# Attention scores of two units at a time as float32 matmuls in the two row halves of TensorE's array, with the step's order on TensorE rewritten

## The reference

```python
q = layernorm(x); k = v = ctx
scores = einsum('bsgrd,btgd->bgrst', xq, xk) / sqrt(64) + mask      # 224 x 750 for each of 8 x 32 heads
probs = softmax(scores)
x = x + tanh(g_xattn) * einsum('bgrst,btgd->bsgrd', probs, xv)
x = x + tanh(g_ffn) * ffn(layernorm(x))                            # routed values, gate from a small MLP
```

## Time and profile before

| | |
|---|---|
| median of 3 runs | 1175.29 us |
| profiled execution | 1174.98 us |
| its span | 1173.1 us |
| TensorE (matmuls) busy | 1150.5 us, 98% |
| VectorE busy | 947.2 us, 81% |
| ScalarE busy | 912.7 us, 78% |
| GpSimd busy | 889.6 us, 76% |
| granted TensorE clock | 0.999 of full |

### The profile page before, as it was taken

How to read it: one execution, slowest core, us unless ns; L and a number is a source line. 1 busy time by engine, 2 the same in 40 slices (tenths; PEclk the granted TensorE clock), 3 DMA queues, 4 the chain that set the end, 5 groups by cost and what they waited for, 6 DMA issues and landing times.

```text
span 1173.1 us, 35389 instructions
## 1 busy us (share of the span) xinstructions
PE 1150.5 (98%) x14656; PEld 907.2 (77%) x14656; DVE 947.2 (81%) x2269; ACT 912.7 (78%) x1226; POOL 889.6 (76%) x804
## 2 busy tenths in 40 slices
PE   5999999999999999999999999999999999999997
PEld 3888888888888888888888888888887655655553
DVE  5888888888888888888888888888874899676775
ACT  5899898888898888898899988898881444655544
POOL 6899999999999999999999999999992110314222
PEclk9999999999999999999999999999999999999999
DMA  9421231133114212411331131122126500012224
GB/s 337 150 69 48 57 117 42 55 75 106 41 43 107 80 49 53 121 42 55 69 111 42 42 73 52 48 53 57 43 79 187 234 2 1 1 59 87 108 99 153
DMA packets 60735, 95.09 MB, mean 81 GB/s; under 512 B 35233, under 2 KB 44449, under 8 KB 56482
## 3 DMA queue, kind: packets, MB, share of 16 engines
q1 hardware_dynamic: 59858, 91.79, 25.7%
q10 hardware_dynamic: 720, 1.05, 0.3%
HBM read 71.75 MB, written 20.97 MB: 79 GB/s over the span
## 4 chain that ended last, share of the span: by engine, by line
PE 76%; POOL 20%; DMA 1%; DVE 1%; issue 1%; ACT 1%; DVEq 0%; SPq 0%; POOLq 0%
POOL arena L593 14%; PE psum L988 13%; PE psum L912 12%; PE psum L935 12%; PE psum L942 6%; PE psum L923 6%; PE psum L965 5%; PE psum L959 5%; PE psum L960 5%; PE psum L1069 3%; POOL arena L560 2%; PE psum L975 2%; PE psum L890 2%; POOL arena L613 1%; PE psum L1038 1%; POOL arena L601 1%
## 5 line engine op out<-in xcount | busy, mean ns | idle before, releaser
L593 POOL TENSOR_TENSOR arena<-arena 128x768 bf16<-128x768 f32 x448 | 651.6, 1469 | 39.7 <-ACT arena L722 37.1
L1312 DVE CUSTOM_DVE_ANT_0 arena<-psum,arena 128x750 f32<-128x750 f32 x448 | 420.3, 938 | 127.1 <-PE psum L923 121.4
L722 ACT ACTIVATE arena<-psum 128x768 f32<-128x768 f32 x448 | 362.3, 809 | 89.4 <-PE psum L942 89.3
L726 ACT ACTIVATE arena<-arena,neg_max 128x750 f32<-128x750 f32 x448 | 410.9, 917 | 3.8 <-DVE neg_max L1312 3.7
L912 PE MATMUL psum<-arena 128*128 128x512 bf16 x896 | 272.1, 384 | 0.8 <-DVE arena L1209 0.8
L935 PE MATMUL psum<-ident,arena 128*128 128x128 f32 x1792 | 268.4, 272 | 0.0
L959 PEld LDWEIGHTS psum<-arena 128*128 128x128 bf16 (+1 forms) x2688 | 194.7, 98 | 57.5
L960 PE MATMUL psum<-arena 128*128 128x64 bf16 (+1 forms) x2688 | 222.0, 193 | 0.0
L959 PE MATMUL psum<-arena 128*128 128x65 bf16 (+1 forms) x2688 | 221.7, 194 | 0.0
L960 PEld LDWEIGHTS psum<-arena 128*128 128x128 bf16 (+1 forms) x2688 | 178.5, 98 | 53.2
L935 PEld LDWEIGHTS psum<-ident,arena 128*128 128x128 f32 x1792 | 206.3, 140 | 4.3
(11 more groups left out here) (166 smaller groups left out, 1301.3 us busy)
## 6 DMA issues: line engine op xcount, KB each, us to landing
arena<-in_k_t SPq DMA_DIRECT2D x128, 187.5 KB, 3.2
arena<-in_v_rows SPq DMA_DIRECT2D x64, 192.0 KB, 2.5
out<-arena SPq DMA_DIRECT2D x12, 1024.0 KB, 3.9
arena<-in_x_top SPq DMA_DIRECT2D x8, 1024.0 KB, 5.4
arena<-in_x_rest SPq DMA_DIRECT2D x8, 768.0 KB, 4.6
spill<-arena SPq DMA_DIRECT2D x96, 64.0 KB, 2.2
arena<-spill SPq DMA_DIRECT2D x6, 1024.0 KB, 10.6
arena<-in_w_t SPq DMA_DIRECT2D x4, 1024.0 KB, 20.4
```

The lines of the kernel that those rows point to most:

```text
L593: pool.tensor_tensor(p_lo[:, n % RING, :], p_sb[:, n % RING, :], high(p_sb[:, n % RING, :]), ALU.subtract).then_inc(p_split, 1)
L722: act.activation(p_sb[:, n % RING, :], flat_ps[:, turned_at(n):turned_at(n) + CW], ACT.Copy).then_inc(evac_a, 1)
L726: act.activation(s_sb[:, n % RING, 0:CTX], s_sb[:, n % RING, 0:CTX], ACT.Exp, bias=neg_max[:, n % 4, :], scale=-1.0).then_inc(exped, 1)
L1312: dve.tensor_tensor_reduce(s_sb[:, n % RING, 0:CTX], flat_ps[:, score_at(n):score_at(n) + CTX], mask_sb[:, max(n % UNITS - REP + 1, 0), :] ...
```

## The change

The scores are now done for two units, a and a+1 (a even), at once, as float32 matmuls without any splitting. The query buffer holds float32, head 2i of a pair of units in rows 0 to 63 and head 2i+1 in rows 64 to 127, as the transposition leaves them; each unit uses one half of the rows as its stationary operand (64 rows), and the copy of the keys that lies in the same rows. The 750 columns of each unit are cut in three steps (238, 274, 238), so placed that at no step the two halves write the same bank; the last block of the odd unit, in bank 1, waits for the even unit's first one (`middle_written`). `k_lo` and its buffer use, `split_k`, `split_q`, `round_q` and their semaphores go; VectorE makes one full-height copy of the turned queries in place of two half copies and two subtractions, for the first pair of groups ScalarE does. So that the units of the second group of each pair find their keys and queries in the same half, the units of that group are taken in exchanged order of heads (`m ^ g % 2`), and the second gathered block is written crossed by two instructions (`crossed`).

TensorE's step is: transposition of unit k+2; in even steps, the scores of units k+4 and k+5; the values of unit k. The odd step has no scores. The scores wait for `maxed` of both units of the pair before. VectorE's reduction waits for both units of its pair. Of each 14 evacuations two (n mod 14 in 1 and 7) go from ScalarE to VectorE.

```diff
+DVE_EVACS = (1, 7)
 def evac_on_dve(n):
-    return False
+    return n % (2 * UNITS) in DVE_EVACS
...
-        k_lo = carve("attention", [128, 2, CTX], BF16)
+        carve("attention", [128, CTX])
-        q_t = carve("attention", [128, 2, 2, UNITS, 128], BF16)
+        q_t = carve("attention", [128, 2, UNITS, 128])
...
+        SCORE_STEPS = ((slice(512, 750), slice(238, 476)), (slice(0, 274), slice(476, 750)), (slice(274, 512), slice(0, 238)))
...
-            def split_k(g):
-                pool.wait_ge(k_loaded[g % 2], 32 * (g // 2 + 1))
-                if g >= 2:
-                    pool.wait_ge(scored, UNITS * (g - 1))
-                pool.tensor_tensor(k_lo[:, g % 2, :], k_raw[:, g % 2, :], high(k_raw[:, g % 2, :]),
-                                   ALU.subtract).then_inc(k_split, 1)
...
+            def score_pair(a):
+                pair, at = divmod(a, 2 * UNITS)
+                for n in (a, a + 1):
+                    g = n // UNITS
+                    if n % UNITS == 0:
+                        pe.wait_ge(k_loaded[g % 2], 32 * (g // 2 + 1))
+                if pair == 0 and at in (0, REP, REP + 2):
+                    pe.wait_ge(q_first, {0: 1, REP: 2, REP + 2: 3}[at])
+                if pair >= 1 and at in (0, REP + 2):
+                    pe.wait_ge(q_copied, 2 * pair - 1 if at == 0 else 2 * pair)
+                if a >= 2:
+                    pe.wait_ge(maxed, a)
+                for i, step in enumerate(SCORE_STEPS):
+                    for half in range(2):
+                        n = a + half
+                        rows, cols = slice(D * half, D * half + D), step[half]
+                        if i == 2 and half == 1:
+                            pe.wait_ge(middle_written, a // 2 + 1)
+                        mm = pe.matmul(flat_ps[:, score_at(n) + cols.start:score_at(n) + cols.stop], q_t[rows, pair % 2, turned_slot(n), :],
+                                       k_raw[rows, n // UNITS % 2, cols], start=True, stop=True)
+                        if i == 0 and half == 0:
+                            mm.then_inc(middle_written, 1)
+                        if i == 2:
+                            mm.then_inc(scored, 1)
...
                 if 0 <= k + 2 < NU:
                     turn_main(k + 2)
                     turn_mid(k + 2)
-                if 0 <= k + 5 < NU:
-                    score_main(k + 5)
+                if k % 2 == 0 and 0 <= k + 4 < NU:
+                    score_pair(k + 4)
                 if k >= 0:
                     value(k)
...
-                if 0 <= k + 5 < NU:
-                    score_mid(k + 5)
-                if k + 5 == 0:
+                if k + 4 == 0:
...
-                    dve.wait_ge(scored, n + 1)
+                    dve.wait_ge(scored, n // 2 * 2 + 2)
+                    if n % 2 == 1 and n >= RING:
+                        dve.wait_ge(turned, n - RING + 1)
...
-                    for half in range(2):
-                        dve.tensor_copy(q_t[D * half:D * half + D, pair % 2, half, turns[0]:turns[-1] + 1, :],
-                                        mix_ps[D * half:D * half + D, (window + 1) % 2, 0:128 * len(turns)].rearrange("p (t n) -> p t n", n=128)
-                                        ).then_inc(q_hi_own, 1)
-                if m in (4, 5) and 1 <= pair < PAIRS:
-                    split_q((window + 1) % 2, pair, m - 4, turn_range(window), 2 * (window + 3) + m - 4 + 1)
+                    dve.tensor_copy(q_t[:, pair % 2, turns[0]:turns[-1] + 1, :],
+                                    mix_ps[:, (window + 1) % 2, 0:128 * len(turns)].rearrange("p (t n) -> p t n", n=128)).then_inc(q_copied, 1)
```

More of the change, by code:

```diff
@@ L61, in evac_on_dve @@
 def evac_on_dve(n):
-    return False
+    return n % (2 * UNITS) in DVE_EVACS
 def evacs_before(n, on_dve):
-    whole, part = divmod(n, UNITS)
-    return sum(whole + (1 if m < part else 0) for m in range(UNITS) if evac_on_dve(m) == on_dve)
+    whole, part = divmod(n, 2 * UNITS)
+    return sum(whole + (1 if m < part else 0) for m in range(2 * UNITS) if evac_on_dve(m) == on_dve)
 def flamingo_block(nc, x_top, x_rest, k_t, v_rows, mask, g_x, av_t, wvd_t, w1_t, wq_t, wr, wr_rows_in, keys_t, log_rel, rel, b1, w2, wvu_t,
@@ L256, in flamingo_block @@
         v_loaded = [sem("v_loaded0"), sem("v_loaded1")]
-        k_split = sem("k_split")
         v_hi_done = sem("v_hi_done")
@@ L260, in flamingo_block @@
         q_turned = sem("q_turned")
-        q_hi_done = sem("q_hi_done")
-        q_hi_own = sem("q_hi_own")
-        q_split = sem("q_split")
+        q_first = sem("q_first")
+        q_copied = sem("q_copied")
+        middle_written = sem("middle_written")
         scored = sem("scored")
@@ L354, in turned_slot, with crossed @@
             if m < REP:
-                return m % 2, (0 if u == 0 else 5) + m // 2
-            return u, 2 + (m - REP)
+                return (0 if u == 0 else 5) + m // 2
+            return 2 + (m - REP)
+        def crossed(cols):
+            return cols.rearrange("p (q a d) -> p q a d", a=2, d=D)
         def turn_range(window):
@@ L362, in flamingo_block @@
         FIRST_BANK = (1, 0, 1)
-        def queries_before(pair):
-            return 4 * pair + 2 if pair else 0
         def evac_wait(eng, n):
@@ L579, in _ @@
             factors(0, top_col)
-            split_k(0)
             root(1, rest_cols)
@@ L585, in _ @@
                 for j in range(NB):
-                    pool.tensor_scalar(xn_rest[:, j, cols], xb[:, 0, j, cols], ln_scale[:, 1 + j:2 + j], ln_bias[:, 1 + j:2 + j],
-                                       ALU.mult, ALU.add).then_inc(done, 1)
+                    scale, bias = ln_scale[:, 1 + j:2 + j], ln_bias[:, 1 + j:2 + j]
+                    if j == 1:
+                        dst, src = crossed(xn_rest[:, j, cols]), crossed(xb[:, 0, j, cols])
+                        pool.tensor_scalar(dst[:, :, 1, :], src[:, :, 0, :], scale, bias, ALU.mult, ALU.add)
+                        pool.tensor_scalar(dst[:, :, 0, :], src[:, :, 1, :], scale, bias, ALU.mult, ALU.add).then_inc(done, 1)
+                    else:
+                        pool.tensor_scalar(xn_rest[:, j, cols], xb[:, 0, j, cols], scale, bias, ALU.mult, ALU.add).then_inc(done, 1)
             for k in range(FIRST, NU):
@@ L594, in _ @@
                                        ALU.subtract).then_inc(p_split, 1)
-                g = window + 2
-                if m == 5 and 1 <= g < GROUPS:
-                    split_k(g)
                 g = window + 1
@@ L694, in norm_rest @@
                 act.wait_ge(ln_done, b + 2)
-                act.activation(xn_rest[:, j, :], xb[:, b % 3, j, :], ACT.Identity, bias=ln_bias[:, 1 + j:2 + j],
-                               scale=ln_scale[:, 1 + j:2 + j]).then_inc(rest_normed, 1)
+                scale, bias = ln_scale[:, 1 + j:2 + j], ln_bias[:, 1 + j:2 + j]
+                if j == 1:
+                    dst, src = crossed(xn_rest[:, j, :]), crossed(xb[:, b % 3, j, :])
+                    act.activation(dst[:, :, 1, :], src[:, :, 0, :], ACT.Identity, bias=bias, scale=scale)
+                    act.activation(dst[:, :, 0, :], src[:, :, 1, :], ACT.Identity, bias=bias, scale=scale).then_inc(rest_normed, 1)
+                else:
+                    act.activation(xn_rest[:, j, :], xb[:, b % 3, j, :], ACT.Identity, bias=bias, scale=scale).then_inc(rest_normed, 1)
             def round_h(t, j):
@@ L702, in round_h, with copy_first @@
                 act.activation(h_hi[:, j], psum[:, j % 2, :].rearrange("p (k n) -> p k n", k=4), ACT.Copy).then_inc(h_hi_done, 1)
[L704 to L710, removed]
-                for half in range(2):
-                    round_q(FIRST_BANK[i], 0, half, FIRST_TURNS[i], i + 1)
+            def copy_first(i):
+                turns = FIRST_TURNS[i]
+                act.wait_ge(q_turned, i + 1)
+                act.activation(q_t[:, 0, turns[0]:turns[-1] + 1, :],
+                               mix_ps[:, FIRST_BANK[i], 0:128 * len(turns)].rearrange("p (t n) -> p t n", n=128), ACT.Copy).then_inc(q_first, 1)
             norm_top(0)
-            round_first(0)
+            copy_first(0)
             for k in range(FIRST, NU):
@@ L739, in _ @@
                 if k in (-3, -2):
-                    round_first(k + 4)
+                    copy_first(k + 4)
                 later = (window - 3) // KV + 1
@@ L862, in turn_first @@
                 if i == 2:
-                    pe.wait_ge(q_split, 2)
+                    pe.wait_ge(q_first, 1)
                 turn_rows(0, FIRST_TURNS[i], FIRST_BANK[i])
@@ L875, in turn_q @@
                     pe.wait_ge(rest_widened, NB)
-                    pe.wait_ge(q_split, 6)
+                    pe.wait_ge(q_first, 3)
                 if window >= 1:
@@ L951, in value @@
                         pe.wait_ge(x_added, g - 1)
-                    pe.wait_ge(q_split, min(2 * g + 6, 4 * PAIRS + 2) if g else 4)
+                    if g == 0:
+                        pe.wait_ge(q_first, 2)
```

(16 more changed lines are left out.)

## The result

The changed kernel takes 1389.37 us (median, 1389.03 to 1389.75), the kernel before beside it 1175.08; the ratio is 1.182, 95% interval 1.180 to 1.184. The profiled execution has a span of 1386.0 us and a granted clock of 1.00. The forecast was 1426 us with a range of 1310 to 1680.

A forecast was written before the change was run, and what follows sets the result against it. TensorE's order was taken to bound the kernel before, a loop over three engines the changed one: 224 x 4.81 = 1078, + 13 + 15 + 8 = 1114 us against 862, giving about 1426 us; range 1310 to 1680.

The forecast's parts named there:

- the loop: Once a pair: scores, maximum, exp, evacuation, transposition, next scores, over TensorE, VectorE and ScalarE; 4.81 us, 224 times.
- TensorE alone: TensorE's own work for a pair of units, without waits: 4.37 us against 3.85 before, 118 us slower in all.
- the rival that they don't: The two halves' score matmuls run one after the other: scores 2.50 us instead of 1.48, 1655 us; chance 27%.
- The rival of perfect overlap: Halves overlap perfectly with free switches, 1332 us, or the evacuation is outside the loop, 1293 us; together 16%.
- scores, 1.48 us: A pair's float32 scores on TensorE: in-order starts give seven slots, 1774 columns, 1.48 us; bounds 1.25 and 2.50.
- The rule on loads: On TensorE a weight load overlaps only another row group's matmuls; each score slot would pay 0.1 us, 157 us.
- The loop's other links: Between scores: VectorE start 0.04, exp 0.98, evacuation 0.81 later, lasting 0.81, TensorE start 0.06, two transposed chunks 0.27 us.
- The additions: Extra work in the loop: v_hi 13 us and the norm 15 us on ScalarE, 64 VectorE evacuations 8 us.
- The changes of height: TensorE switching between 128 and 64 rows around a pair's scores: 0.19 us in, 0.15 out, bounds 0 and 0.2 each.
- the other loop: The way over both maxima and an add_part on VectorE: 3.2 us, hidden within 0.2.
- GpSimd was the true bound: Rival: GpSimd set the time and loses 1.44 of 12.7 us a window; 11 us less, 1164 us; chance 3%.
- The rival on the clock: TensorE's granted clock falls to 1.2 GHz in the new waits: over 900 us more; chance 2%.

The follow-up runs named there:

- half after half: Changed kernel with the six score matmuls reordered, half 0 three times, then half 1 three times: 1494.84 us.
- The small matmuls: Changed kernel with scores before the transposition, plus one two-column float32 matmul ahead of odd steps' values: 1369.48 us with 64 rows, 1316.15 with 128.

## Why the prediction was right, and where it was off

**What bounds it, and the loop.** The mechanism was right, by the runs with scores first, values first, all evacuations on ScalarE and ScalarE's extra work moved, each of which moves the time the way the loop has it, three of them within 3 us of the size that it gives and the first within 20 us of the interval. Of the 214 us the loop is 99 (1389 against 1290). The other 115 (1290 against 1175) are TensorE's own work, except for the 13 us in which it waits for the second maximum and the 4.7 ahead of the first group of value matmuls (29.4 against 24.7). The forecast had 118 for TensorE alone (224 x 0.52 is 116). That the two sums agree is luck: errors cancel in it (below).

**The halves overlap.** They do, and the trace shows it: the rival that they don't, at 27%, falls. The rival of perfect overlap, at 16%, was right on the overlap and wrong on the rest, for the switches are not free and the evacuation does stand in the loop. The Trainium skill, TensorEngine Tiling (Array Packing), Key Properties, has tiles that operate independently; this trace agrees, with starts 0.007 us apart. Two narrow windows of the changed kernel, the first passes of both halves and, later, the last four:

```profile
507.93 0.47 PE L904 MATMUL psum<-arena 64*128 64x238 f32 x2
508.90 0.57 PE L904 MATMUL psum<-arena 64*128 64x238 f32 x4
```

**The mis-sized term: scores, 1.48 us.** I took it that instructions start in the program's order, so that one half's first pass waits for the other half's first one to end: seven slots. The first row above has two records that together last 0.47 us, as long as one of them: both halves start at once (0.007 us apart in the single records). So there are six slots, 1500 x 0.833 = 1.25 us of columns. With an uncovered load of 0.107 and the tail of 0.17 that is 1.53, measured 1.54; the forecast had 0.10 + 1.48 + 0.17 = 1.75. 0.21 x 224 = 47 us. The other links together are 0.03 longer than forecast, which leaves 0.18 a pair, 40 us; VectorE's evacuations were 3 us too dear, and the start phase, where I had 1 us less, took 4.5 more. That is the miss of 37 us. My lower bound was the truth, and the reason for choosing 1.48 above it was an assumption on order that no row bore. The run with half after half shows in another way that matmuls of the two halves do not start in the order of kernel.py. In what order the passes were queued the trace does not say.

**The rule on loads.** The Trainium skill, TensorE: Matmul & The Clock Gate, Part 3, has a load overlap only with another row group's matmuls; the prediction made 157 us of it. The trace disagrees: twelve passes fit into 1.54 us, which leaves room for one bare load. In the run with half after half, half 0 is alone at first, so that no other row group is at work. Its second load lies at 504.042 to 504.228 us, while its first pass still streams (the second starts at 504.240), and that second pass takes 0.201 us to the next start, which is its 238 columns.

**The loop's other links.** VectorE's start 0.07 (0.04), exp 0.99 (0.98), evacuation 0.83 (0.81) and its length 0.79 (0.81), TensorE's start 0.05 (0.06): all within 0.03. From turn_mid's start to the first pass of the scores 0.36, forecast 0.27 + 0.09 (the load stands in the scores' 1.54). The guess that the evacuation, not the exp, ends last is in the waits (59 + 31 us for L714, 24 for L1291, 41 for the exp, for which turn_main waits ahead of that).

**The additions.** v_hi 0.42 in 32 pairs: 0.41 (5.04 against 4.63). The norm 0.70 in 22: 0.70 (5.33). Together 28 us, forecast 28, measured 28. VectorE's evacuations 0.13 in 64 pairs: 0.08, 5 us instead of 8 (6 by the run without them). That query transpositions hide in the loop: they do, the pairs with and without them take 4.63 us alike where all evacuations are on ScalarE.

**The changes of height.** The forecast had 0.19 in and 0.15 out. In the loop only the way in counts: 0.09 empty ahead of the first pass and 0.11 of load, in sum 0.20 ("0.17 <-issue" is the idle time of the load queue, which begins earlier). The way out is hidden by the loop and open in the kernel with the scores first: 0.09 empty behind the last pass and 0.05 more in the first transpositions, about as forecast. The small matmuls give 0.28 for both. The Trainium skill, TensorEngine Tiling (Array Packing), Key Properties, says that a change of tiling mode drains TensorE; the 0.09 us that stand empty ahead of the scores agree.

**TensorE alone.** Forecast 4.37 us a pair; with the true 1.25 it would have been 4.14, and 4.03 without the query transpositions. The kernel with the scores first has 4.34 on the mean and 4.17 in plain pairs. So TensorE's sum lacked 0.12 for the transpositions of the odd step, which I had put at 0.66 as before, and 0.07 on the mean for the pair in seven that waits for VectorE's second maximum. Against them stood the 0.23 too much for the scores. The second maximum is the other loop that I had set down as hidden; it was, as long as the first was there.

**What freed engines bring.** Nothing, as forecast: GpSimd's 92 us, VectorE's 116 and ScalarE's 52 went into waits. "GpSimd was the true bound" (3%) falls with its idle time, 332 us. The rival on the clock (2%) falls too: the granted clock is 1.00 over the whole span.

No version here beats the kernel before. The best order of the new work needs 4.17 us for a plain pair, and the kernel before 3.73. The float32 scores stream no longer than the bf16 ones (1.25 against 1.30), but come with some 0.3 us of empty time and bare load around them, and the transpositions of both steps take 0.17 more. A version with the scores first and ScalarE's extra work in odd steps together was not tried.

## What to carry to other kernels

When work of two units is put together to use an engine better, ask first how long the result now has until its consumer: here three steps became two, and the way over three engines did not fit. Draw the loop "result, next engine, next, back to this engine" with what stands in each engine's queue between the links, and hold it against the engine's own sum; the larger one is the time. The order of the same instructions was worth 99 us in one direction and cost 124 us in the other, and an instruction on ScalarE, which is busy for less than two thirds of the time, cost its full length as soon as it stood inside the loop.

## What the hardware showed that I had not expected

Two float32 matmuls on 64 rows each, one after the other in the program, start 0.007 us apart, though each is two passes: the columns of a pair stream in 1.25 us, where end to end they would take 2.50. With three matmuls of half 0 ahead of it, half 1 starts 0.51 us late, beside half 0's second matmul and before its third: it passes part of what stands before it in kernel.py. Going from 128 to 64 rows and back costs 0.28 us with next to no work between, wherever TensorE sets the time.
